# A group norm with channel attention: order of the high and value passes in the first pair and in steady passes, a statistics chain of four steps, and a last store in two halves from two queues

## Chip, cores and metric

The kernel runs on one core of a Trainium2 chip. The metric is the device time of one execution in microseconds, the median of several runs.

## What is computed

The input x has 16 images of 192 channels and 48 x 48 = 2304 positions. Per image, in eight heads of d = 24 channels:

```python
xn = _gn(x)                                  # 32 groups of 6 channels, eps 1e-5
qkv = tokens(xn) @ w_qkv                     # 2304 x 192 @ 192 x 576
q = q / norm(q, over the 2304 tokens)        # per channel
k = k / norm(k, over the 2304 tokens) * temperature
attn = softmax(k^T q, axis=-1)               # 24 x 24 per head
out = (attn applied to v) @ w_out + b_out
return x + out
```

## The kernel before, in words

Images go in pairs (8 pairs). Three tiles t hold a pair's 384 channels on 128 partitions: t = 0 and 2 the upper 128 channels of the two images, t = 1 the lower 64 of both. The normalised x is held as a sum of two 16-bit parts: `h_sb` (high) and `l_sb` (low = value - high). Attention between channels needs only the Gram matrix of the tokens, so the kernel computes, for a pair, the Gram matrix (`g_ps`), from it T = G W (`tq`, high and low), scores and norms, the softmax, V (`vh`, `vl`) and one folded matrix M (`mh0`, `mh1`, `ml0`, `ml1`) that is multiplied with the normalised x and added to x.

The work runs in nine steps p = -1 to 7, each written for all five engines at once. Step p has a first half A, 18 slots of 128 tokens, in which TensorE transposes tokens of pair p+1 into PSUM, ScalarE copies them (`tok`, line 613) and TensorE multiplies them into the Gram matrix, three slots behind; between slots stand the softmax, V and M of pair p. Its second half B has 18 results of pair p (384 columns each, VectorE line 938), and between them the small steps T, products, scores of pair p+1. The normalisation of pair p+2 runs beside both: in nine chunks of 768 columns, each needs a value pass `x<c>` (`xn`, line 566, a ring of three buffers), a high pass `h<c>` (line 575), both on ScalarE, and a low pass on GpSimd (line 503), which waits for both. The value passes 0 to 2 of the second pair are VectorE's (`second_value`, line 789). A value pass c must wait until low pass c-3 has read its buffer.

All engines execute in order. The order is written by hand in tables: `*_PE_A`, `*_ACT_A`, `*_VEC_A` give what stands behind which slot of half A, `*_B` what stands in half B; `FIRST_` is step -1, `SECOND_` step 0, `LAST_` step 7, the others are steady. `flip`, `v` and `m` on TensorE are the transposes of the scores, the V product and the M product. On VectorE `soft_in` (lines 853 to 858) needs `flip`; `exp` on ScalarE (line 619) needs the end of `soft_in`; `soft_out` (866 to 875) needs `exp`. `spread` (line 843) needs the powers that GpSimd takes of the norms (line 520).

Statistics: VectorE's `bn_stats` pieces (line 799) wait for a load of x; `channel_stats` (807 to 818) makes three 16-bit parts of mean and mean square, which TensorE sums over groups. SyncE issues loads, stores (line 408) and the copies `hl` of a tile's halves.

Of the kernel before, what the change touches and what calls it, by code (L numbers as in the profile page):

```python
# [107 lines left out]
def preact_attention(nc, x, w_qkv, temperature, w_out, b_out, ident, ident16, groups, headmask, out):  # L108
# [30 lines left out]
    with ExitStack() as ctx:  # L139
        def sb(name, shape, dt=F32):  # L140
            return ctx.enter_context(nc.sbuf_tensor(name, shape, dt))
# [218 lines left out]
        def _(sp):  # L360
# [355 lines left out]
        @block.vector
        def _(dve):
# [64 lines left out]
            def second_value(c):  # L782
# [164 lines left out]
            def step(p):  # L947
# [31 lines left out]
                for j in range(SLOTS):  # L979
                    for what in hooks(p, FIRST_VEC_A, VEC_A, LAST_VEC_A, PAIRS - 1).get(j, ()):  # L980
# [7 lines left out]
                    pieces(now, 0 if first else BN_A.get(j, 0))
                assert not now
                for n in range(NO):  # L990
                    if small:
                        result(p, n)
                    for what in hooks(p, FIRST_VEC_B, VEC_B, LAST_VEC_B, PAIRS - 2).get(n, ()):
# [406 lines left out]
```

## Time and profile before

| | us |
|---|---|
| median of 3 runs | 352.33 (351.12 to 352.65) |
| profiled execution, its own time | 350.15 |
| its span, first to last instruction | 348.4 |
| TensorE busy | 310.9 (89%) |
| VectorE busy | 284.4 (82%) |
| ScalarE busy | 242.9 (70%) |
| GpSimd busy | 145.8 (42%) |
| half A of step 0 begins | about 53 |
| first steady step begins | about 96 |

Times in the trace are from the start of the span. The device time holds 1.75 us around the span. A busy share is an average over stages; what a change in one stage is worth is read from the waits of that stage. PE is TensorE, PEld its weight loads, DVE VectorE, ACT ScalarE, POOL GpSimd, SP SyncE. The granted clock of TensorE is 0.988 of its full speed on the mean.

### The profile page before, as it was taken

The numbers are of one execution on the slowest core, as the hardware profiler recorded it, in microseconds if no ns is written. First come the engines' busy times: TensorE is split into PE (matmuls) and PEld (weight loads), VectorE is DVE, ScalarE is ACT, GpSimd is POOL, SyncE is SP. The second block draws the span as 40 slices with busy tenths as digits, with TensorE's granted clock in tenths as the row PEclk, the third lists the DMA queues.
The fourth block names the chain that finished last, engine by engine and source line by source line (L and its number), as shares of the span: only waits on it lengthen the run. The fifth ranks groups of instructions, "written<-read, shape, count | busy, mean of one in ns | idle before, by whom it ended". The sixth has DMA issues, their size and how long they took to land.

```text
span 348.4 us, 9368 instructions
## 1 busy us (share of the span) xinstructions
PE 310.9 (89%) x3692; PEld 221.8 (64%) x3692; DVE 284.4 (82%) x705; ACT 242.9 (70%) x447; POOL 145.8 (42%) x129
## 2 busy tenths in 40 slices
PE   0039858999999999999999999999999999999895
PEld 0027736765678667866787567866787568856552
DVE  5999894896999689986998699968998685278874
ACT  1089689867997599759996699759986899640300
POOL 0059679303870178315750287115930586002000
PEclk9999987999999999999999999999999999999999
DMA  7999920004995279915994399627992574016876
GB/s 225 355 322 259 246 77 2 3 1 144 301 350 164 92 208 349 301 52 169 305 310 127 119 292 328 216 93 186 320 322 63 154 235 132 3 48 181 283 215 229
DMA packets 30828, 67.75 MB, mean 194 GB/s; under 512 B 5504, under 2 KB 12096, under 8 KB 30784
## 3 DMA queue, kind: packets, MB, share of 16 engines
q1 hardware_dynamic: 30544, 66.56, 61.3%
q10 hardware_dynamic: 240, 0.59, 0.6%
q8 instruction: 29, 0.48, 0.6%
q14 instruction: 15, 0.12, 0.1%
HBM read 29.38 MB, written 28.31 MB: 166 GB/s over the span
## 4 chain that ended last, share of the span: by engine, by line
PE 72%; ACT 8%; issue 7%; DVE 6%; SPq 2%; DMA 2%; POOL 2%; ACTq 0%; POOLq 0%; DVEq 0%
PE u_ps L1015 29%; PE g_ps L1015 20%; PE s_ps L1015 10%; PE u_ps L1066 4%; PE u_ps L1067 4%; ACT tok L613 3%; ACT h_sb L575 2%; DMA wo<-in_L_conv_w_out_dram 2%; PE u_ps L1068 2%; PE u_ps L1069 2%; ACT xn L566 2%; DVE x_sb L938 1%; SPq L381 1%; POOL l_sb L503 1%; SPq L386 1%
## 5 line engine op out<-in xcount | busy, mean ns | idle before, releaser
L503 POOL TENSOR_TENSOR l_sb<-xn,h_sb 128x768 f16<-128x768 f32 x63 | 103.2, 1652 | 49.3 <-ACT h_sb L575 49.3
L938 DVE SCALAR_TENSOR_TENSOR x_sb<-u_ps,bias,x_sb 128x384 f32<-128x384 f32 x144 | 83.7, 610 | 13.6 <-PE u_ps L1015 13.0
L1015 PE MATMUL g_ps<-tok 128*128 128x64 f16 (+1 forms) x864 | 86.4, 240 | 4.1 <-ACT tok L613 4.0
L613 ACT COPY tok<-u_ps 128x384 f32<-128x384 f32 x144 | 65.7, 484 | 17.3 <-PE u_ps L1069 16.0
L799 DVE BATCH_NORM_STATS2 bnst<-x_sb 128x6 f32<-128x384 f32 x144 | 71.5, 545 | 4.0 <-DMA x_sb<-in_x_dram 3.9
L1015 PEld LDWEIGHTS g_ps<-tok 128*128 128x128 f16 x864 | 57.2, 99 | 27.5 <-ACT tok L613 6.5
L1015 PE MATMUL u_ps<-h_sb,ml 128*128 128x384 f16 (+1 forms) x336 | 72.7, 326 | 0.0
L566 ACT ACTIVATE xn<-x_sb,rb 128x768 f32<-128x768 f32 x60 | 59.6, 1026 | 14.0 <-POOL rb L515 14.0
L575 ACT ACTIVATE h_sb<-x_sb,rb 128x768 f16<-128x768 f32 x63 | 64.3, 1034 | 0.4 <-POOL rb L515 0.4
L1066 PE MATMUL u_ps<-id,h_sb 128*128 128x128 f16 x288 | 49.2, 224 | 6.1 <-DVE l_sb L779 5.3
L1067 PE MATMUL u_ps<-id,l_sb 128*128 128x128 f16 x288 | 49.2, 224 | 0.0
L1015 PE MATMUL u_ps<-hl,mh 128*128 128x384 f16 (+1 forms) x192 | 47.5, 330 | 0.1
L1015 PE MATMUL u_ps<-h_sb,mh 128*128 128x384 f16 (+1 forms) x192 | 47.1, 326 | 0.0
L509 POOL TENSOR_TENSOR grs<-gvar,minus_half 128x3 f32<-128x3 f32 x8 | 7.1, 882 | 95.6 <-DVE gvar L832 95.6
L1015 PE MATMUL u_ps<-l_sb,mh 128*128 128x384 f16 (+1 forms) x192 | 47.1, 326 | 0.0
L1015 PEld LDWEIGHTS u_ps<-h_sb,ml 128*128 128x128 f16 (+1 forms) x336 | 28.7, 101 | 20.1 <-issue 3.0
L1069 PE MATMUL u_ps<-id,l_sb 128*128 128x128 f16 x144 | 32.3, 224 | 0.0
L1068 PE MATMUL u_ps<-id,h_sb 128*128 128x128 f16 x144 | 32.3, 224 | 0.0
L1066 PEld LDWEIGHTS u_ps<-id,h_sb 128*128 128x128 f16 x288 | 27.5, 100 | 6.7 <-ACT h_sb L582 5.4
L1067 PEld LDWEIGHTS u_ps<-id,l_sb 128*128 128x128 f16 x288 | 28.9, 100 | 0.4
L1015 PEld LDWEIGHTS u_ps<-hl,mh 128*128 128x128 f16 (+1 forms) x192 | 14.7, 103 | 11.9 <-issue 3.1
L520 POOL TENSOR_TENSOR r<-n,minus_half 96x8 f32<-96x8 f32 x8 | 13.6, 1700 | 18.7 <-DVE n L837 18.7
(149 smaller groups left out, 527.0 us busy)
## 6 DMA issues: line engine op xcount, KB each, us to landing
x_sb<-in_x_dram SPq DMA_DIRECT2D x48, 384.0 KB, 5.5
out_dram<-x_sb SPq DMA_DIRECT2D x48, 384.0 KB, 3.5
out_dram<-x_sb SPq DMA_DIRECT2D x48, 192.0 KB, 3.2
x_sb<-in_x_dram SPq DMA_DIRECT2D x45, 192.0 KB, 5.0
hl<-h_sb SPq DMA_DIRECT2D x48, 96.0 KB, 3.2
hl<-l_sb SPq DMA_DIRECT2D x48, 96.0 KB, 3.4
x_sb<-in_x_dram ACTq DMA_DIRECT2D x3, 192.0 KB, 4.2
w<-in_L_conv_w_qkv_dram SPq DMA_DIRECT2D x1, 288.0 KB, 7.2
```

Source lines behind the costliest of these rows:

```text
L503: nc.gpsimd.tensor_tensor(l_sb[:, par, t, cols], xn[:, c % XN_RING, :], h_sb[:, par, t, cols], ALU.subtract).then_inc(l_ok, 1)
L520: nc.gpsimd.tensor_tensor(r8[:, :], n8[:, :], minus_half[0:HC, :].to_broadcast([HC, 8]), ALU.pow).then_inc(r8_ok, 1)
L566: nc.scalar.activation(xn[:, c % XN_RING, :], xcol(q, t, g * GW, GW), ACT.Identity, bias=rb[:, par, 1, t:t + 1], scale=rb[:, par, 0, t:t + ...
L575: nc.scalar.activation(h_sb[:, par, t, g * GW:g * GW + GW], xcol(q, t, g * GW, GW), ACT.Identity, bias=rb[:, par, 1, t:t + 1], scale=rb[:, ...
L613: nc.scalar.copy(tok[:, j % TOK_RING, :, :].rearrange("p b n -> p (b n)").bitcast(F32), slot_words(j)).then_inc(tok_a, 1)
L799: ins = V.bn_stats(bnst[:, t, 6 * part:6 * part + 6], xcol(q, t, part * BW, BW))
L938: V.scalar_tensor_tensor(out=xs, in0=block_ps(n), scalar=bias[:, t:t + 1], in1=xs, op0=ALU.add, op1=ALU.add).then_inc(out_ok, 1)
L1015: return nc.tensor.matmul(dst, lhs, rhs, start=start, stop=stop, skip_group_check=True)
L1066: nc.tensor.transpose(bank[:, b, 0:P], h_sb[:, par, 2 * b, px], id16[:, 0:P])
L1067: nc.tensor.transpose(bank[:, b, 256:384], l_sb[:, par, 2 * b, px], id16[:, 0:P])
L1068: nc.tensor.transpose(bank[:, :, P:P + C1], h_sb[:, par, 1, px], id16[:, 0:P])
L1069: nc.tensor.transpose(bank[:, :, P + C1:P + 2 * C1], l_sb[:, par, 1, px], id16[:, 0:P]).then_inc(tr_mm, 1)
```

## The change

Six things are edited. (1) In steady steps ScalarE's h7 moves from slot 4 to behind exp in slot 5, and h8 from slot 7 to slot 8. (2) In step -1 ScalarE takes T's high parts ahead of h2, and VectorE its third value pass behind T. (3) In step 0 the value passes 6 and 7 go from ScalarE to VectorE, so that h6, h7 and h8 come earlier on ScalarE, and flip, v and m stand two, one and one slots earlier on TensorE. (4) `channel_stats` keeps the moments as 32-bit numbers whose upper halves TensorE reads as the 16-bit parts: four dependent steps in place of six. (5) The last store, of tile 1 and the last 768 columns, is cut in two halves of 384 columns, each started as its result is done; SyncE issues the first image's part, ScalarE the second's. (6) The waits of GpSimd and of the ring follow (3).

```diff
-ACT_A = {1: ["h6"], 3: ["x8"], 4: ["h7"], 5: ["exp"], 7: ["h8"], 11: ["v"], 14: ["m"]}
+ACT_A = {1: ["h6"], 3: ["x8"], 5: ["exp", "h7"], 8: ["h8"], 11: ["v"], 14: ["m"]}
...
-FIRST_ACT_B = ["h0", "h1", "h2", "t2", "t0", "t1", "x3", "p", "h3", "x4", "h4", "x5"]
+FIRST_ACT_B = ["h0", "h1", "t2", "t0", "t1", "h2", "x3", "p", "h3", "x4", "h4", "x5"]
...
-FIRST_VEC_B = {0: ["var", "gram", "wm", "v0", "v1", "z", "v2", "t2", "t0"],
-               1: ["t1", "lo", "bn", "norms", "wo", "spread", "bn", "bn", "bn"]}
+FIRST_VEC_B = {0: ["var", "gram", "wm", "v0", "v1", "z", "t2", "t0"],
+               1: ["t1", "v2", "lo", "bn", "norms", "wo", "spread", "bn", "v6", "bn", "bn"]}
...
-SECOND_PE_A = {3: ["flip"], 10: ["v"], 13: ["m"]}
-SECOND_ACT_A = {0: ["h5"], 1: ["x6"], 2: ["h6"], 3: ["x7"], 4: ["h7"], 5: ["x8"], 6: ["exp"], 7: ["h8"], 12: ["v"], 15: ["m"]}
+SECOND_PE_A = {1: ["flip"], 9: ["v"], 12: ["m"]}
+SECOND_ACT_A = {0: ["h5"], 1: ["h6"], 2: ["h7"], 4: ["x8"], 5: ["exp", "h8"], 12: ["v"], 15: ["m"]}
+SECOND_VEC_A = {**VEC_A, 0: ["soft_in", "v7"]}
...
                 ch.then(V.tensor_tensor(mv[:, :, 1], mv[:, :, 1], msq[:, :], ALU.add))
-                ch.then(V.tensor_copy(parts[:, 0, :, :], mv[:, :, :]))
-                ch.then(V.tensor_tensor(res1[:, :, :], mv[:, :, :], parts[:, 0, :, :], ALU.subtract))
-                ch.then(V.tensor_copy(parts[:, 1, :, :], res1[:, :, :]))
-                ch.then(V.tensor_tensor(parts[:, 2, :, :], res1[:, :, :], parts[:, 1, :, :], ALU.subtract))
+                for k in (0, 1):
+                    ch.then(V.tensor_tensor(moments[:, k + 1, :, :], moments[:, k, :, :], parts[:, k, :, :], ALU.subtract))
...
+                        if p == PAIRS - 1 and k == NC_ - 1:
+
+                            for i in (0, 1):
+                                sp.wait_ge(out_ok, done[k] - 1 + i)
+                                chip, dram = ends([c + i * BW for c in at[g]], image, o_d, t, g * GW + i * BW, BW)[0]
+                                sp.dma_start(dram, chip).then_inc(stored[t][g], 16)
...
+            def last_store():
+                t, g = ROWS[-1]
+                q = PAIRS - 1
+                for i in (0, 1):
+                    c = g * GW + i * BW
+
+                    act.wait_ge(out_ok, (q + 1) * NO + NO - 1 + i)
+                    act.dma_start(o_d[2 * q + 1:2 * q + 2, P:C, c:c + BW].rearrange("o c n -> (o c) n"),
+                                  xcol(q, t, c, BW)[C1:P, :]).then_inc(stored[t][g], 16)
...
-                V.tensor_scalar(xn[:, c, :], xcol(1, t, g * GW, GW), rb[:, 1, 0, t:t + 1], rb[:, 1, 1, t:t + 1],
+
+                need(dve, l_ok, c + 1 - XN_RING)
+                V.tensor_scalar(xn[:, c % XN_RING, :], xcol(1, t, g * GW, GW), rb[:, 1, 0, t:t + 1], rb[:, 1, 1, t:t + 1],
```

ScalarE in a steady half A, from x8 to the copies behind h8; `tok` is a token copy, `xn` a value pass, `h_sb` a high pass, `s_ps` with 96x96 the exp. Before:

```order
L566 ACTIVATE xn<-x_sb,rb 128x768
L613 COPY tok<-u_ps 128x384
L575 ACTIVATE h_sb<-x_sb,rb 128x768
L613 COPY tok<-u_ps 128x384
L619 ACTIVATE s_ps<-s_ps 96x96
L613 COPY tok<-u_ps 128x384 x2
L575 ACTIVATE h_sb<-x_sb,rb 128x768
L613 COPY tok<-u_ps 128x384 x4
```

With the change:

```order
L575 ACTIVATE xn<-x_sb,rb 128x768
L622 COPY tok<-u_ps 128x384 x2
L628 ACTIVATE s_ps<-s_ps 96x96
L584 ACTIVATE h_sb<-x_sb,rb 128x768
L622 COPY tok<-u_ps 128x384 x3
L584 ACTIVATE h_sb<-x_sb,rb 128x768
L622 COPY tok<-u_ps 128x384 x3
```

The high pass that stood between two token copies now stands behind exp, and three copies follow it before h8 in place of two.

ScalarE in half A of step 0, from the first token copy's successor h5 on. Before:

```order
L575 ACTIVATE h_sb<-x_sb,rb 128x768
L613 COPY tok<-u_ps 128x384
L566 ACTIVATE xn<-x_sb,rb 128x768
L613 COPY tok<-u_ps 128x384
L575 ACTIVATE h_sb<-x_sb,rb 128x768
L613 COPY tok<-u_ps 128x384
L566 ACTIVATE xn<-x_sb,rb 128x768
L613 COPY tok<-u_ps 128x384
L575 ACTIVATE h_sb<-x_sb,rb 128x768
L613 COPY tok<-u_ps 128x384
L566 ACTIVATE xn<-x_sb,rb 128x768
L613 COPY tok<-u_ps 128x384
```

With the change:

```order
L584 ACTIVATE h_sb<-x_sb,rb 128x768
L622 COPY tok<-u_ps 128x384
L584 ACTIVATE h_sb<-x_sb,rb 128x768
L622 COPY tok<-u_ps 128x384
L584 ACTIVATE h_sb<-x_sb,rb 128x768
L622 COPY tok<-u_ps 128x384 x2
L575 ACTIVATE xn<-x_sb,rb 128x768
L622 COPY tok<-u_ps 128x384
L628 ACTIVATE s_ps<-s_ps 96x96
L584 ACTIVATE h_sb<-x_sb,rb 128x768
```

The value passes x6 and x7 are gone from between the token copies, the high passes have moved up, and behind exp stands h8 at once.

VectorE from the end of step -1 into step 0, from `spread` (`qk_s`) to the softmax; `xn` is a value pass. Before:

```order
L843 TENSOR_TENSOR qk_s<-s_ps,r 96x384
L799 BN_STATS bnst<-x_sb 128x6 x3
L853 TENSOR_TENSOR lg<-s_ps,mask 96x384
L855 TENSOR_REDUCE s_ps<-lg 96x96
L856 TENSOR_TENSOR s_ps<-s_ps,rk 96x96
L857 TENSOR_REDUCE mx<-s_ps 96x4
L858 TENSOR_TENSOR s_ps<-s_ps,mx 96x96
```

With the change:

```order
L863 TENSOR_TENSOR qk_s<-s_ps,r 96x384
L821 BN_STATS bnst<-x_sb 128x6
L811 TENSOR_SCALAR xn<-x_sb,rb 128x768
L821 BN_STATS bnst<-x_sb 128x6 x2
L873 TENSOR_TENSOR lg<-s_ps,mask 96x384
L875 TENSOR_REDUCE s_ps<-lg 96x96
L876 TENSOR_TENSOR s_ps<-s_ps,rk 96x96
L877 TENSOR_REDUCE mx<-s_ps 96x4
L878 TENSOR_TENSOR s_ps<-s_ps,mx 96x96
L811 TENSOR_SCALAR xn<-x_sb,rb 128x768
L821 BN_STATS bnst<-x_sb 128x6 x2
```

Value pass 6 now stands between the statistics pieces ahead of the softmax, and value pass 7 directly behind its last step.

## Rows read from the trace of the kernel before

**Rows 1.** The page: the chain that ended last, by engine.

```profile
PE 72%; ACT 8%; issue 7%; DVE 6%; SPq 2%; DMA 2%; POOL 2%; ACTq 0%; POOLq 0%; DVEq 0%
```

**Rows 2.** Windows: stretch, its length, busy us of PE, PEld, DVE, ACT, POOL, clock, DMA.

```profile
96.00:134.00 38.00, 37.75 (x464) 27.25 (x464) 33.02 (x84) 31.18 (x57) 17.94 (x15) 1.00 0.68 220
...
172.00:210.00 38.00, 37.37 (x459) 26.71 (x456) 32.45 (x82) 30.89 (x56) 17.27 (x15) 1.00 0.71 228
```

**Rows 3.** Waits from 58 to 96 us: total us, times, longest.

```profile
PEld g_ps L1015 <- ACT tok L613: 3.3, 7, 0.8
```

**Rows 4.** Timeline of TensorE, steady pass: start, us, instruction; Gram products 3, 4, 5.

```profile
99.83 0.60 PE L1015 MATMUL g_ps<-tok 128*128 128x384 f16 x6
...
100.60 0.60 PE L1015 MATMUL g_ps<-tok 128*128 128x384 f16 x6
...
101.79 0.62 PE L1015 MATMUL g_ps<-tok 128*128 128x384 f16 x6 [0.25 <-ACT tok L613]
```

**Rows 5.** Timeline of ScalarE at the same place: h7, token copy 5, exp.

```profile
100.31 1.06 ACT L575 ACTIVATE h_sb<-x_sb,rb 128x768 f16<-128x768 f32 x1
101.24 0.50 ACT L613 COPY tok<-u_ps 128x384 f32<-128x384 f32 x1
101.60 0.26 ACT L619 ACTIVATE s_ps<-s_ps 96x96 f32<-96x96 f32 x1
```

**Rows 6.** Timelines of VectorE (last softmax step) and GpSimd (low part 8).

```profile
100.51 0.26 DVE L858 TENSOR_TENSOR s_ps<-s_ps,mx 96x96 f32<-96x96 f32 x1
...
103.63 1.64 POOL L503 TENSOR_TENSOR l_sb<-xn,h_sb 128x768 f16<-128x768 f32 x1 [0.55 <-ACT h_sb L575]
```

**Rows 7.** Timeline of ScalarE, end of step -1: h3, first token copy of pair 1.

```profile
51.35 1.03 ACT L575 ACTIVATE h_sb<-x_sb,rb 128x768 f16<-128x768 f32 x1
...
55.04 0.46 ACT L613 COPY tok<-u_ps 128x384 f32<-128x384 f32 x1
```

**Rows 8.** VectorE: value passes (ns min/median/max, first and last start), spread, softmax's last step.

```profile
L789 DVE TENSOR_SCALAR xn<-x_sb,rb x3: 673/678/1732, 45.2 to 46.6; 128x768 f32<-128x768 f32 x3
...
56.08 0.55 DVE L843 TENSOR_TENSOR qk_s<-s_ps,r 96x384 f32<-96x384 f32 x1 [1.22 <-POOL r L520]
...
62.77 0.26 DVE L858 TENSOR_TENSOR s_ps<-s_ps,mx 96x96 f32<-96x96 f32 x1
```

**Rows 9.** Timeline of ScalarE, step 0: token copy 6, exp.

```profile
62.77 0.48 ACT L613 COPY tok<-u_ps 128x384 f32<-128x384 f32 x1
63.12 0.26 ACT L619 ACTIVATE s_ps<-s_ps 96x96 f32<-96x96 f32 x1
```

**Rows 10.** Timeline of TensorE, step 0: Gram products 6, 8, transposes 12, product 16, first result.

```profile
63.30 0.61 PE L1015 MATMUL g_ps<-tok 128*128 128x384 f16 x6 [0.34 <-ACT tok L613]
...
65.13 0.61 PE L1015 MATMUL g_ps<-tok 128*128 128x384 f16 x6
...
66.58 0.22 PE L1066 MATMUL u_ps<-id,h_sb 128*128 128x128 f16 x1
...
74.79 0.39 PE L1015 MATMUL g_ps<-tok 128*128 128x384 f16 x3 [0.68 <-ACT tok L613]
...
75.68 0.33 PE L1015 MATMUL u_ps<-h_sb,mh 128*128 128x384 f16 x1
```

**Rows 11.** Timeline of VectorE, step 3: last statistics step, first result.

```profile
190.87 0.17 DVE L818 TENSOR_TENSOR parts<-res,parts 128x6 bf16<-128x6 f32 x1
191.07 0.62 DVE L938 SCALAR_TENSOR_TENSOR x_sb<-u_ps,bias,x_sb 128x384 f32<-128x384 f32 x1
```

**Rows 12.** The end: last result, the two stores' issue, landing of the later one, a window.

```profile
344.06 0.62 DVE L938 SCALAR_TENSOR_TENSOR x_sb<-u_ps,bias,x_sb 128x384 f32<-128x384 f32 x1 [0.30 <-PE u_ps L1015]
...
344.71 1.11 SPq L408 DMA_DIRECT2D out_dram<-x_sb  x2
...
DMA to landing us min/median/max: 2.7/2.7/2.7
...
345.70:347.40 1.70, 0.00 (x0) 0.00 (x0) 0.00 (x0) 0.00 (x0) 0.00 (x0) 0.80 0.89 231
```

More of the change, by code:

```diff
@@ L90 @@
 POOL_SECONDS = (3, 5)
-BY_VECTOR_1 = 3
-SECOND_PE_A = {3: ["flip"], 10: ["v"], 13: ["m"]}
-SECOND_ACT_A = {0: ["h5"], 1: ["x6"], 2: ["h6"], 3: ["x7"], 4: ["h7"], 5: ["x8"], 6: ["exp"], 7: ["h8"], 12: ["v"], 15: ["m"]}
+BY_VECTOR_1 = (0, 1, 2, 6, 7)
+SECOND_PE_A = {1: ["flip"], 9: ["v"], 12: ["m"]}
+SECOND_ACT_A = {0: ["h5"], 1: ["h6"], 2: ["h7"], 4: ["x8"], 5: ["exp", "h8"], 12: ["v"], 15: ["m"]}
+SECOND_VEC_A = {**VEC_A, 0: ["soft_in", "v7"]}
 LAST_PE_A = {0: ["m"]}
@@ L174, in preact_attention @@
         bnst = sb("bnst", [P, 3, NB * 6])
-        mv = sb("mv", [P, 3, 2])
+        moments = sb("moments", [P, 3, 3, 2])
+        mv = moments[:, 0, :, :]
         msq = sb("msq", [P, 3])
-        parts = sb("parts", [P, 3, 3, 2], BF16)
-        res1 = sb("res1", [P, 3, 2])
-        res2 = sb("res2", [P, 3, 2])
+        parts = moments[:, :, :, :].rearrange("p a t s -> p (a t s)").bitcast(BF16).rearrange(
+            "p (a t s h) -> p a t s h", a=3, t=3, s=2)[:, :, :, :, 1]
         gsum = sb("gsum", [P, 3, 2])
@@ L311, in preact_attention @@
         out_ok = sem("out_ok")
-        STAT, GVAR, NORM, SOFT, ATTN = 6, 4, 2, 5, 6
+        STAT, GVAR, NORM, SOFT, ATTN = 4, 4, 2, 5, 6
         def high_count(k):
@@ L404, in step @@
                         t, g = ROWS[k]
-                        sp.wait_ge(out_ok, done[k])
-                        for chip, dram in ends(at[g], image, o_d, t, g * GW, GW):
-                            sp.dma_start(dram, chip).then_inc(stored[t][g], 16)
+                        if p == PAIRS - 1 and k == NC_ - 1:
[3 more added lines that the diff above has]
+                                sp.dma_start(dram, chip).then_inc(stored[t][g], 16)
+                        else:
+                            sp.wait_ge(out_ok, done[k])
+                            for chip, dram in ends(at[g], image, o_d, t, g * GW, GW):
+                                sp.dma_start(dram, chip).then_inc(stored[t][g], 16)
                     if more and k >= LOAD_LAG:
@@ L455, in _ @@
             for t, g in ROWS:
-                sp.wait_ge(stored[t][g], PAIRS * (32 if t == 1 else 16))
+                sp.wait_ge(stored[t][g], PAIRS * (32 if t == 1 else 16) + (32 if (t, g) == ROWS[-1] else 0))
         @block.gpsimd
@@ L498, in split @@
                     pool.wait_ge(h_ok, (q - 1) * NC_ + c + 1)
-                    if q == 1 and c < BY_VECTOR_1:
-                        pool.wait_ge(xn1_vec, c + 1)
-                    else:
-                        pool.wait_ge(xn_ok, (q - 1) * NC_ + c + 1 - BY_VECTOR_1)
+                    if q == 1 and c in BY_VECTOR_1:
+                        pool.wait_ge(xn1_vec, BY_VECTOR_1.index(c) + 1)
+                    else:
+                        by_vector = len(BY_VECTOR_1) if q > 1 else sum(k < c for k in BY_VECTOR_1)
+                        pool.wait_ge(xn_ok, (q - 1) * NC_ + c + 1 - by_vector)
                     nc.gpsimd.tensor_tensor(l_sb[:, par, t, cols], xn[:, c % XN_RING, :], h_sb[:, par, t, cols],
@@ L711, in step @@
                         small_steps[what](p + 1)
+            def last_store():
[6 more added lines that the diff above has]
+                                  xcol(q, t, c, BW)[C1:P, :]).then_inc(stored[t][g], 16)
             for_pairs(act, step)
+            last_store()
         @block.vector
@@ L979, in step @@
                 for j in range(SLOTS):
-                    for what in hooks(p, FIRST_VEC_A, VEC_A, LAST_VEC_A, PAIRS - 1).get(j, ()):
+                    for what in hooks(p, FIRST_VEC_A, VEC_A, LAST_VEC_A, PAIRS - 1, SECOND_VEC_A).get(j, ()):
                         if what == "stats":
@@ L985, in step @@
                             pieces(now, 1)
+                        elif what == "v7":
+                            second_value(7)
                         elif small:
@@ L1002, in step @@
                             mixed_weights()
-                        elif what in ("v0", "v1", "v2"):
+                        elif what in ("v0", "v1", "v2", "v6"):
                             second_value(int(what[1]))
```

## Prediction

> **What bounds the kernel now.** I read the page first. In its chain of what ended last TensorE holds 72% of the span, and no other engine more than 8% [rows 1]. The windows say where this holds: in a steady pass (96 to 134 us) TensorE is busy 37.75 of 38 us [rows 2]. So there only the gaps between matmuls can be won. In the pass of pair 0 the list of waits has the weight loads of Gram products waiting 3.3 us for ScalarE's copies of transposed tokens (`tok`), in 7 places [rows 3]. A steady pass has one such place. Gram products follow each other every 0.77 us (99.83, 100.60), but the one after is due at 101.38 and starts at 101.79 [rows 4]. ScalarE started the copy for it at 101.24, since a high part (h7, 0.93 us) stood ahead of it from 100.31 [rows 5]. Six steady passes (pairs 1 to 6) repeat this. The end is another stage: after VectorE's last result at 344.06 only the store is left [rows 12].
>
> **The change, part by part.** All sums are in the profiled execution, whose own time is 350.15 us for a span of 348.4; the median of the runs shown is 352.33 (351.12 to 352.65). I take the change in us from the one and subtract it from the other.
>
> *Steady passes: h7 goes behind exp, h8 one slot back.* Gram product 5's copy now starts at 100.31 and ends by 100.8: its 0.41 us wait is gone. Then comes exp. It needs VectorE's last softmax step, which starts at 100.51 and takes 0.26 [rows 6], so it ends at 100.77 and exp starts at some 100.86, where ScalarE stood free since 100.67. After it, exp holds the engine for 0.16 (0.26 in its row, less the 0.1 by which pieces overlap there) and h7 for 0.93 [rows 5]: the copy for Gram product 6 starts at 101.95 and, at 0.48, ends at 102.43. Product 6 is due at 101.38 + 0.77 = 102.15 and starts at 102.48. So a wait of 0.41 turns into one of 0.33: the stall moves by one product, 0.08 us is won, 0.5 in six passes. h8 then stands at some 103.03 and its low part on GpSimd at 104.1 in place of 103.63, ending 0.5 us later at 105.75 [rows 6]; the transposes that need it come behind Gram product 9 at about 106.2, so this costs nothing, with 0.45 us of cover left. Bounds: all 0.41 six times (2.5 us) if exp finds its input ready, a loss of 0.1 per pass if the copy is later than I count. I keep 0.5, since the row of the softmax step is that close.
>
> *First pass, T's high parts ahead of h2.* ScalarE has the same seven pieces and must wait for TensorE's T instead of running h2 in between. By my count the third product is cast by 51.4 as before, h3 starts at 51.38 against 51.35 and the first token copy at 55.07 against 55.04 [rows 7]. VectorE's part: of its three value passes the third (v2, at 46.6) took 1.73 us, as GpSimd's first low part ran beside it; the two before took 0.67 and 0.68 [rows 8]. Behind T it meets an idle GpSimd and should take 0.68. But GpSimd's third low part waits for v2 and ends at about 52.7; GpSimd has then another low part (1.64) before the power for the norms, which starts at 54.3, by my count 0.25 later than before. Sum for TensorE: 0 (the second pair's transposes are fed from copies at 55.04 either way), between -0.3 and +0.5.
>
> *Pass of pair 0.* ScalarE loses two value passes (x6, x7: 1.86 us), VectorE gets them (v6, v7), and h6, h7 come earlier. Step by step: the norms' spread on VectorE at 56.34 (was 56.08 [rows 8]); a statistics piece 0.47; v6 at 57.3, where GpSimd is in a low part (56.5 to 58.2). As with v2 I let v6 wait for its end and finish 0.42 later, at 58.6. Two pieces more and the softmax starts at 59.5. Its five steps take 2.3, so it ends at 61.8, where before its last step started at 62.77 and ended at 63.03 [rows 8]. ScalarE: token copies at 0.36 and three high parts bring it to x8 at 59.65; x8 needs GpSimd's sixth low part, at 60.15; the copy for product 5 starts at 61.1, exp at 61.87 (was 63.12 [rows 9]), h8, the copy for product 6 at 62.96 (was 62.77 [rows 9]), ending 63.44. So Gram product 6 starts at 63.5 against 63.30 [rows 10]: no gain yet. But then ScalarE holds nothing but copies. Before, the stretch from product 6 to the first result (75.68) was 12.38 us, in which TensorE waited 0.26 at product 8 (65.13, where two steps of 0.78 behind 63.30 make 64.87), 0.22 ahead of the transposes at 66.58, which want the last low part, and 0.68 for a copy queued behind M's high parts (74.79) [rows 10]. With low part 8 done at 65.6, and M's products two slots earlier in the same stretch (one slot for V's), these three are gone: 63.5 + 12.38 - 1.16 = 74.7. Gain 1.0 us, between 0.3 (v6 and v7 both meet a fresh low part of 1.64 us, and exp is late by as much) and 1.8 (neither does).
>
> Here the Trainium skill (SBUF — State Buffer, "Who interferes with whom") says that GpSimd and a VectorE instruction in a two-port mode lock each other out of a shared pair for a whole instruction, whichever starts second. The 1.73 against 0.68 us of the value pass agrees. By that rule v6 or v7, once started, also pushes GpSimd's next low part back by its own length.
>
> *Statistics chain, 6 steps to 4.* A step costs 0.20 (190.87 to 191.07 [rows 11]), so 0.41 per pass. In the head the first one is covered: the weights' load holds VectorE and ScalarE anyway; the second ends as TensorE reaches it, worth 0.05. In steady passes VectorE waits for the first result, so 0. Once, in the pass of pair 3, a load came late and the chain ran into the first result: 190.87 is followed by the result at 191.07 with no idle time [rows 11], and TensorE's busy time in that pass is 37.37 of 38 us in place of 37.75 [rows 2]. There up to 0.41 comes back, if the load is late again: I count 0.3.
>
> *Last stores.* After the last result (344.06 + 0.62) SyncE issued two DMAs, 1.11 us for both from 344.71; the later one landed 2.7 us after its start of 345.2, and data moved from 345.7 to 347.4 [rows 12]. Now half of it leaves 0.9 us earlier, and the last half is issued by two queues at once, at 344.75. With half the bytes, data moves from 345.7 for some 0.85 us, so the end comes 0.8 us earlier. Bounds: 0.5 (only the second issue is saved) to 1.3.
>
> The Trainium skill (SBUF — State Buffer, "Can I just issue two DMAs to hit both halves?") speaks against the second queue: two DMAs at partitions 0 and 64 share the same engines and serialize. By it the transfer is that half of 1.7 us, the 0.8 above; if they ran side by side it would be 1.2. No row here has two queues storing at once.
>
> Sum: 0.5 + 0 + 1.0 + 0.05 + 0.3 + 0.8 = 2.65 us. 352.33 - 2.65 = 349.7 us.
>
> **Rivals.**
> 1. *The value passes are not held.* v6 takes 0.68 in a gap of GpSimd; the softmax is 0.7 us earlier, x8 starts 0.3 earlier, product 6 starts at 62.8: 0.7 more, 349.0. For it: GpSimd's rows have gaps. Against: it has five low parts in a row there, and v2 met one.
> 2. *The gains vanish into new waits.* In pass 0 ScalarE stands still at exp with all token copies queued behind it; if v6 and v7 cost VectorE 1 us more, pass 0 gives 0.3, and the steady passes 0. Left are the tail and little else: 1.2 us, 351.1. For it: rows 6 leave exp only 0.1 us.
> 3. *Slower: exp holds the token copies in every pass.* ScalarE is in order, and exp now stands ahead of h7 without cover; before, h7 hid up to 0.8 us of softmax lateness (100.77 to 101.60). With lateness d the loss is d in each of seven passes. From d = 0.35 all of the 2.65 is gone, and at d = 0.65 it is 354.3, slower by over 0.5%. Against: the softmax hangs on the flip, which stands early in TensorE's order and waits for no copy of this pass.
> 4. *The change does less than it says:* the loads are on time (0 for 0.3), and the halves of the store serialize behind each other's issue (0.5): 350.3. This lies inside the main range.
>
> **How the numbers follow.** A change of 0.5% is 1.76 us, about what a measurement of this kernel can tell from none. Forecast as summed (with 4): 0.58, range 348.6 to 350.9. Rival 1: 0.14. Rival 2: 0.20. Rival 3: 0.08. Of the first, some 0.1 lies under 1.76 us of gain. Faster: 0.58 - 0.06 + 0.14 + 0.04 = 0.70; slower: 0.05; same: 0.25. The range that leaves out 2 in 10 reaches from 347.9 (rival 1 with a full tail and a fourth of the 2.5 that a steady pass could give at most) to 351.6 (rival 2 and half of its spread). 349.7 is the likeliest, not the mean.
>
> **What would show it.** Steady pass: the waiting Gram product is the one after h7, with a wait of 0.33, and a pass takes 0.08 us less. Pass 0: v6 or v7 longer than 1 us; Gram product 6 at about 63.5, first result at 74.7. v2 at 0.68 us and the first token copy at 55.0. Last store: two issues in two queues at the same time, the span's end 3.7 - 0.8 = 2.9 us after the last result. It is wrong if exp's input comes late in steady passes, if low part 8 stops the transposes, or if the head's copies start later than 55.1.

## The result, and the profile after

The changed kernel's median was 347.02 us (346.39 to 347.58, 4 runs) beside 351.73 for the kernel before (350.56 to 352.65, 4 runs); ratio 0.9867, 95% interval 0.9827 to 0.9908. Two later comparisons of the same pair gave 0.9894 (0.9853 to 0.9935) and 0.9910 (0.9878 to 0.9942). Over all comparisons of this study the changed kernel has 18 runs with a mean of 347.55 and the kernel before 101 runs with a mean of 351.03: **3.5 us faster, give or take 0.5** (two standard errors). I had forecast 349.7 (347.9 to 351.6), a gain of 2.65; both 347.02 and 347.55 lie under that range.

The profiled execution took 346.39 us for a span of 344.6. The page's chain that ended last has hardly moved: TensorE still holds it [rows 1].

```profile
PE 71%; DVE 9%; ACT 8%; issue 5%; DMA 2%; SPq 2%; POOL 2%; ACTq 0%; POOLq 0%; DVEq 0%
```

**Steady pass**, windows of two whole passes, from the first transposes of one pair to those of the next (the first line is the same cut in the kernel before; [rows 2] has it at other places):

```profile
96.08:133.92 37.84, 37.59 (x463) 27.16 (x462) 32.86 (x83) 31.12 (x56) 17.78 (x15) 1.00 0.68 219
...
94.69:132.37 37.68, 37.60 (x462) 27.16 (x461) 32.44 (x81) 31.12 (x56) 17.79 (x15) 1.00 0.71 222
132.37:170.06 37.69, 37.61 (x463) 27.15 (x462) 32.55 (x81) 31.13 (x56) 17.79 (x15) 1.00 0.69 215
```

TensorE works as long as before (37.60 for 37.59 us) and stands idle for 0.08 in place of 0.25. Gram products 4 to 6 in the first of the two passes [rows 4]:

```profile
99.21 0.60 PE L1037 MATMUL g_ps<-tok 128*128 128x384 f16 x6
...
99.99 0.60 PE L1037 MATMUL g_ps<-tok 128*128 128x384 f16 x6
...
101.00 0.61 PE L1037 MATMUL g_ps<-tok 128*128 128x384 f16 x6
```

ScalarE and VectorE there: exp, h7, token copy 6, and the softmax step that exp waits for [rows 5, 6]:

```profile
99.42 0.23 ACT L628 ACTIVATE s_ps<-s_ps 96x96 f32<-96x96 f32 x1
99.57 1.02 ACT L584 ACTIVATE h_sb<-x_sb,rb 128x768 f16<-128x768 f32 x1
100.49 1.22 ACT L622 COPY tok<-u_ps 128x384 f32<-128x384 f32 x3
...
99.13 0.26 DVE L878 TENSOR_TENSOR s_ps<-s_ps,mx 96x96 f32<-96x96 f32 x1
```

Products 4 and 5 follow each other in 0.78 us, product 6 comes after 1.01: the stall has moved to product 6, as forecast, but it is 0.24 us and not 0.33. The softmax step ends at 99.39 and exp starts at 99.42, 0.03 us later, where I had allowed 0.09. It is the same 0.03 in all six steady passes.

**Pass of pair 0**, Gram products 5 and 6 and the first result on TensorE, v6, the softmax's last step and v7 on VectorE, and two of GpSimd's low parts [rows 8 to 10]:

```profile
61.48 0.61 PE L1037 MATMUL g_ps<-tok 128*128 128x384 f16 x6
63.25 0.61 PE L1037 MATMUL g_ps<-tok 128*128 128x384 f16 x6 [0.82 <-ACT tok L622]
...
74.36 0.33 PE L1037 MATMUL u_ps<-h_sb,mh 128*128 128x384 f16 x1
...
57.18 1.31 DVE L811 TENSOR_SCALAR xn<-x_sb,rb 128x768 f32<-128x768 f32 x1
...
61.37 0.26 DVE L878 TENSOR_TENSOR s_ps<-s_ps,mx 96x96 f32<-96x96 f32 x1
61.54 0.67 DVE L811 TENSOR_SCALAR xn<-x_sb,rb 128x768 f32<-128x768 f32 x1
...
58.04 1.95 POOL L512 TENSOR_TENSOR l_sb<-xn,h_sb 128x768 f16<-128x768 f32 x1
...
62.36 1.64 POOL L512 TENSOR_TENSOR l_sb<-xn,h_sb 128x768 f16<-128x768 f32 x1 [0.75 <-DVE xn L811]
```

v6 was held beside GpSimd (1.31 us), v7 was not (0.67). One large stall is left, ahead of product 6, and behind it the copies keep pace: the first result starts at 74.36 (before 75.68 [rows 10]). Counted from the pass's first transposes (53.05 before, 52.99 now), product 6 starts at 10.25 us before and 10.26 now. So the gain of 1.33 lies behind product 6, as forecast: 1.27 up to the first result, the rest in the second half.

What lets the softmax start earlier is the flip. In the kernel before, VectorE was idle and waited for it:

```profile
60.74 0.55 DVE L853 TENSOR_TENSOR lg<-s_ps,mask 96x384 f32<-96x384 f32 x1 [2.73 <-PE s_ps L1194]
```

With the change this step starts at 59.35 and no longer waits. My prediction had the time right without naming this wait. No run takes the flip's move and that of the value passes apart.

**The end**, last result and the halves on two queues [rows 12]:

```profile
341.05 0.62 DVE L958 SCALAR_TENSOR_TENSOR x_sb<-u_ps,bias,x_sb 128x384 f32<-128x384 f32 x1 [0.29 <-PE u_ps L1037]
...
341.70 0.47 SPq L412 DMA_DIRECT2D out_dram<-x_sb  x1
341.70 0.50 ACTq L729 DMA_DIRECT2D out_dram<-x_sb  x1
...
DMA to landing us min/median/max: 2.1/2.1/2.1
...
DMA to landing us min/median/max: 2.4/2.4/2.4
```

Both last halves are issued at 341.70 and land after 2.1 us (SyncE's) and 2.4 us (ScalarE's). The span ends 3.55 us after the last result's start, before it was 4.34; spans are read to 0.1 us. Data of the last halves moved in this window (before, in [rows 12], the last data moved from 345.7 to 347.4):

```profile
342.80:343.70 0.90, 0.00 (x0) 0.00 (x0) 0.00 (x0) 0.00 (x0) 0.00 (x0) 1.00 0.78 219
```

### The profile page after: what moved, and what is told of

The parts are those of the page before. It is cut to its first block, busy times and chain, and to the rows that moved or that the text cites. A ratio compares the mean times of both kernels' runs of the same rounds, so it can differ in the third digit from the quotient of the medians.

```text
span 344.6 us, 9354 instructions
## 1 busy us (share of the span) xinstructions
PE 310.7 (90%) x3692; PEld 222.6 (65%) x3692; DVE 282.4 (82%) x691; ACT 241.8 (70%) x445; POOL 146.0 (42%) x129
## 4 chain that ended last, share of the span: by engine, by line
PE 71%; DVE 9%; ACT 8%; issue 5%; DMA 2%; SPq 2%; POOL 2%; ACTq 0%; POOLq 0%; DVEq 0%
PE u_ps L1037 33%; PE g_ps L1037 17%; PE s_ps L1037 12%; ACT tok L622 4%; ACT h_sb L584 3%; PE u_ps L1088 3%; PE u_ps L1089 3%; DMA wo<-in_L_conv_w_out_dram 2%; DVE bnst L821 2%; PE u_ps L1091 1%; PE u_ps L1090 1%; DVE l_sb L799 1%; DVE s_ps L786 1%; DVE xn L811 1%; SPq L382 1%
## 5 line engine op out<-in xcount | busy, mean ns | idle before, releaser
L512 POOL TENSOR_TENSOR l_sb<-xn,h_sb 128x768 f16<-128x768 f32 x63 | 103.1, 1653 | 51.5 <-ACT h_sb L584 49.1
L622 ACT COPY tok<-u_ps 128x384 f32<-128x384 f32 x144 | 64.2, 482 | 17.3 <-PE u_ps L1091 16.2
L575 ACT ACTIVATE xn<-x_sb,rb 128x768 f32<-128x768 f32 x58 | 57.5, 1026 | 14.4 <-POOL rb L524 14.0
```

What stands on the lines that cost most here:

```text
L512: nc.gpsimd.tensor_tensor(l_sb[:, par, t, cols], xn[:, c % XN_RING, :], h_sb[:, par, t, cols], ALU.subtract).then_inc(l_ok, 1)
L575: nc.scalar.activation(xn[:, c % XN_RING, :], xcol(q, t, g * GW, GW), ACT.Identity, bias=rb[:, par, 1, t:t + 1], scale=rb[:, par, 0, t:t + ...
L622: nc.scalar.copy(tok[:, j % TOK_RING, :, :].rearrange("p b n -> p (b n)").bitcast(F32), slot_words(j)).then_inc(tok_a, 1)
```

## The experiments

All comparisons are with the kernel before unless a line says otherwise. "First transposes" are those of each pair; their starts cut a trace into passes. The table has every trace but those of the three kernels with added steps or delayed loads, which come further down. Columns: start of the first transposes of pair 0; time from there to pair 1's (first pass); to pair 2's (pass of pair 0); the five steady passes that follow; last result's start to the end of the span (to 0.05, since spans are read to 0.1).

```
kernel       head   first  pair 0  steady passes (pairs 1 to 5)      end
before       23.86  29.19  43.03   37.84 37.84 38.51 37.84 37.83     4.34
e_same       23.70  29.19  43.30   37.84 37.84 37.83 37.84 37.84     4.31
e_chain      25.26  29.19  42.99   37.85 37.86 37.85 37.86 37.85     4.27
e_store      23.91  29.20  43.14   37.86 37.86 38.35 37.86 37.87     3.53
e_steady     25.20  29.20  43.05   37.68 37.69 37.67 37.68 37.68     4.30
e_pass0      24.08  29.19  41.54   37.85 37.84 38.85 38.02 37.85     4.26
e_first      23.75  29.23  44.04   37.85 37.84 39.21 37.84 38.18     4.33
e_first2     23.83  29.26  43.00   37.86 37.84 37.84 38.35 38.56     4.25
after        23.72  29.27  41.70   37.68 37.69 37.68 37.69 37.67     3.55
e_after2     25.95  29.27  41.67   37.66 37.67 37.66 37.66 37.66     3.55
e_after3     25.15  29.26  41.70   37.68 37.68 38.36 37.68 37.68     3.47
e_nofirst    25.07  29.20  41.48   38.36 37.68 37.67 38.67 37.68     3.54
best1        25.00  29.27  41.67   37.41 37.66 37.97 38.04 37.41     3.47
best2        24.12  29.26  41.41   37.41 37.41 37.42 40.75 37.42     3.51
best3        24.44  29.20  41.32   37.42 37.42 37.42 37.48 37.43     3.57
```

**Each part alone: e_chain, e_store, e_steady, e_pass0.** Each is the kernel before with one part of the diff and nothing else.

```diff
e_chain: STAT 6 -> 4, the parts read from moments' upper halves
e_store: the last k of SyncE's step in halves, last_store() on ScalarE
e_steady:
-ACT_A = {1: ["h6"], 3: ["x8"], 4: ["h7"], 5: ["exp"], 7: ["h8"], ...
+ACT_A = {1: ["h6"], 3: ["x8"], 5: ["exp", "h7"], 8: ["h8"], ...
e_pass0: BY_VECTOR_1, SECOND_PE_A, SECOND_ACT_A, SECOND_VEC_A, "v6" as in the change
```

> The kernel before with the statistics chain of four steps alone. Additive theory (each part gives what the two profiles show at its place): where loads are on time the chain is covered in every steady pass, the head gives 0.05 us, and only a pass with a late load gives up to 0.41; so 0 to 0.5 us below the kernel before, with pass starts as before except in a pass with a late load. Rival theory (the chain is what makes the medians differ by 4.7 where the profiles differ by 3.8): late loads come in several passes of ordinary runs, each gives up to 0.41, and the chain alone is worth 1 us or more.

Measured: ratio 0.9973 (0.9953 to 0.9994). In its trace no pass differs from those of before, where no load cost anything, by more than 0.04. The timed runs don't decide: the interval reaches from 0.2 to 1.7 us, and so takes in both theories.

> The kernel before with the last store in halves over two queues alone. Additive theory: 0.8 us below the kernel before, all of it after the last result (4.34 us from the last result's start to the span's end become 3.55, as in the profile of the changed kernel), and every pass start where it was. Rival: the second queue brings nothing or the end waits for the slower queue, 0.3 or less.

Measured: 0.9958 (0.9937 to 0.9980), 1.5 us by the ratio; in the trace the end took 3.53 us, 0.81 less than before. This run has halves and second queue together.

> The kernel before with h7 moved behind exp and h8 one slot back in the steady passes alone. Theory (the softmax's end wakes exp after 0.03 us, so the one stall shrinks from 0.41 to 0.24): 37.68 us per steady pass in place of 37.84, about 1.0 us in six passes. My prediction's count: 0.08 per pass, 0.5 in all. Rival (the 0.16 belongs to other parts, such as the shorter chain): 0 to 0.3 us.

Measured: 0.9971 (0.9946 to 0.9995); 37.68 in each of five passes, 0.16 less. That is all of the steady passes' gain in the changed kernel, so neither the chain nor another part has a share in it.

> The kernel before with the new order of the pass of pair 0 alone (x6 and x7 on VectorE as v6 and v7, the flip, V's and M's products earlier). Theory: 1.3 us, all between the first transposes of pair 1 and those of pair 2 (43.03 us become 41.7), nothing in the steady passes. My prediction's count: 1.0. Rival (part of that gain hangs on the earlier start that the first pass's reorder and the shorter chain give): 0.8 or less alone.

Measured: 0.9939 (0.9915 to 0.9964); the pass of pair 0 took 41.54 us, 1.49 less, more than in the changed kernel (41.70). The traces bear out the additive theory at each place. By the means of the timed runs the four parts add up to 5.7 us in place of 3.5. All four stand against the same 33 runs of the kernel before, whose mean (351.37) is 0.34 above that of all 101: four times that is 1.4 of the 2.2 us too many. The next runs ask what the comparison itself gives.

**The same kernel again: e_same, e_after2.**

> The kernel before, unchanged, run once more as if it were a changed one. It measures what the comparison itself gives: 0, give or take 0.7 us. The four parts run alone came out 1.25, 1.5, 1.0 and 2.0 us below the kernel before in their means, 5.7 in all, where the whole change gives 4.4 to 4.7. If this copy is also some 0.3 to 0.5 us below, that surplus is the comparison's own. Its trace also shows once more whether the pass of pair 3 runs into a late load (38.5 us or more in place of 37.84).

Measured: 0.9987 (0.9959 to 1.0014), by this ratio 0.45 us in its own favour, within the noise; no late load cost anything in its trace.

> The changed kernel once more, in more runs. Theory that the profiles tell all (3.8 us between the two profiled executions, and the 4.7 of the medians is spread): 3.8 or a little above. Theory that ordinary runs of the kernel before lose more to late loads than the profiled one did, and the four-step chain absorbs it: 4.4 or more, with the changed kernel's own runs closer together than those of before.

Measured: 0.9894, 3.7 us. Its trace shows why single runs stray: the head starts 2.2 us later than in the first trace of the same kernel. First the changed kernel's trace, then e_after2's; ScalarE's first cast of weights and TensorE's first transposes:

```profile
17.08 0.52 ACT L599 ACTIVATE wh<-w 128x384 f16<-128x384 f32 x1 [12.84 <-DMA wo<-in_L_conv_w_out_dram]
...
23.72 0.26 PE L1088 MATMUL u_ps<-id,h_sb 128*128 128x128 f16 x1 [5.25 <-DVE l_sb L799]
```

```profile
19.31 0.52 ACT L599 ACTIVATE wh<-w 128x384 f16<-128x384 f32 x1 [15.08 <-DMA wo<-in_L_conv_w_out_dram]
...
25.95 0.26 PE L1088 MATMUL u_ps<-id,h_sb 128*128 128x128 f16 x1 [5.25 <-DVE l_sb L799]
```

Between the two lines lie 6.64 us in both, and in every trace of the table. The weights' landing alone moves the start by 2.23, in kernels with and without the change (23.70 to 25.26 and 23.72 to 25.95 in the table). The span of e_after2 is 2.1 longer, and all of it is there. So the first comparison's 4.7 us, from four runs each, held about a microsecond of luck.

**The chain's slack: e_longchain, e_late6, e_late4.** The first has four more dependent steps.

```diff
-        STAT, GVAR, NORM, SOFT, ATTN = 6, 4, 2, 5, 6
+        STAT, GVAR, NORM, SOFT, ATTN = 10, 4, 2, 5, 6
...
+                for _ in range(4):
+                    ch.then(V.tensor_copy(res2[:, :, :], mv[:, :, :]))
```

> The kernel before with a statistics chain of ten steps in place of six (four more dependent copies, 0.82 us per pass). Theory: in a steady pass the chain has about 0.5 us of slack ahead of the first result, so each of the passes with a chain inside loses some 0.3 us more, 1.5 to 2 in the steady ones, 0.8 to 1.6 in the head, where a chain stands on the path: 2.5 to 3.5 us slower, and late loads then cost their full length. Rival (the chain never reaches the path in steady passes, so that the four-step chain can't have given anything there): slower by the head alone, 0.8 to 1.6 us.

Measured: 1.0101 (1.0069 to 1.0134), by this ratio 3.5 us slower; in its trace the first pass and the pass of pair 0 together took 1.4 more. VectorE ahead of the first result, in the kernel before and then in e_longchain:

```profile
113.90 0.17 DVE L818 TENSOR_TENSOR parts<-res,parts 128x6 bf16<-128x6 f32 x1
114.61 0.62 DVE L938 SCALAR_TENSOR_TENSOR x_sb<-u_ps,bias,x_sb 128x384 f32<-128x384 f32 x1 [0.55 <-PE u_ps L1015]
```

```profile
155.60 0.17 DVE L818 TENSOR_TENSOR parts<-res,parts 128x6 bf16<-128x6 f32 x1
155.80 0.79 DVE L820 COPY res<-mv 128x6 f32<-128x6 f32 x4
156.62 0.62 DVE L940 SCALAR_TENSOR_TENSOR x_sb<-u_ps,bias,x_sb 128x384 f32<-128x384 f32 x1
```

The idle 0.55 us is gone. The cleanest steady passes took 38.26 and 38.29 us, 0.42 and 0.45 more for 0.82 added, so the six-step chain had about 0.4 us of slack. (In these two passes VectorE also waited 0.2 and 0.3 us for a load; counted in, the slack is 0.6 to 0.7. So it is known as 0.4 to 0.7, and the idle 0.55 lies between.) The next two issue one load later in each pass, one with six steps and one with four:

```diff
-                    done_group = {2: 0, 5: 1, NC_ + LOAD_LAG - 1: 2}.get(k)
+                    done_group = {2: 0, 5: 1, NC_ + LOAD_LAG - 2: 2}.get(k)
```

> The kernel before, with the last load of each pair issued behind four copies of the queue in place of ahead of them (2.5 us of issues), so that it is late in every steady pass; chain of six steps. The ten-step chain took 0.43 us of its 0.82 from each on-time pass, so the chain has 0.4 us of slack. Theory: each pass loses the lateness less 0.4, some 1 to 2 us in each of five passes.

> The same late loads with the statistics chain of four steps. Theory (the two steps are slack that late loads eat): each late pass loses 0.41 us less than with six steps, 1.6 to 2.1 us less in all. Rival (the four-step chain gives nothing behind a late load, since VectorE's queue or the first result sets the restart): within 0.5 us of the six-step one.

Measured: 1.0104 (1.0060 to 1.0147) and 1.0060 (1.0032 to 1.0088): by the ratios the four-step chain is 1.5 us better behind late loads (1.8 by the medians), with intervals that overlap. How much a pass waits for its load is read in VectorE's waits. Here two of them, e_late6 from 252 to 270 us and e_late4 from 176 to 193:

```profile
DVE bnst L799 <- DMA x_sb<-in_x_dram: 1.6, 1, 1.6
```

```profile
DVE bnst L799 <- DMA x_sb<-in_x_dram: 2.9, 4, 1.1
```

Set against what the pass lost over 37.84 us, the five passes of each read:

```
e_late6 (six steps)   waited 2.0 0.8 1.3 1.6 1.6   lost 1.64 0.34 0.80 1.14 1.03   absorbed 0.36 to 0.57
e_late4 (four steps)  waited 0.2 0.7 2.9 1.2 2.8   lost 0.00 0.01 2.16 0.33 1.86   absorbed 0.74 to 0.94
```

(The last column leaves out the two waits that cost nothing.) The means are 0.47 and 0.85, 0.38 apart, for two steps removed of 0.41 us: in steady passes they add slack and nothing else. They pay only where the waits of a pass are longer than about 0.4, then up to 0.4. Other traces agree: the wait of 1.1 in the pass of pair 3 cost the kernel before 0.67, in the changed kernel a wait of 0.8 cost nothing.

**The first pass's new order: e_first, e_first2, e_nofirst.**

```diff
-FIRST_ACT_B = ["h0", "h1", "h2", "t2", "t0", "t1", "x3", ...
+FIRST_ACT_B = ["h0", "h1", "t2", "t0", "t1", "h2", "x3", ...
-FIRST_VEC_B = {0: [..., "z", "v2", "t2", "t0"], 1: ["t1", "lo", ...
+FIRST_VEC_B = {0: [..., "z", "t2", "t0"], 1: ["t1", "v2", "lo", ...
```

e_nofirst is the changed kernel with these lines as they were.

> The kernel before with the new order of T's high parts, the third high piece and the third value pass alone. The trace of the changed kernel has 29.27 us from the first transposes of pair 0 to those of pair 1 in place of 29.19. Theory (additive): the same 0.08 us more here, nothing elsewhere, so a result within the comparison's noise of 0.7 us. Rival (it is what lets the pass of pair 0 start its norms and softmax as it does): the pass of pair 0 changes by 0.3 us or more either way.

Measured: 1.0012 (0.9985 to 1.0039), and 44.04 us in the pass of pair 0. I had not foreseen a loss of 1.0. The windows show the clock. Kernel before, then e_first:

```profile
50.00:56.00 6.00, 5.18 (x70) 4.75 (x71) 4.39 (x10) 5.50 (x8) 5.00 (x3) 0.50 0.01 3
57.00:64.00 7.00, 5.62 (x75) 4.01 (x74) 4.14 (x11) 7.00 (x13) 5.76 (x4) 1.00 0.00 1
```

```profile
50.00:54.00 4.00, 2.70 (x66) 2.54 (x63) 3.62 (x8) 4.00 (x7) 2.94 (x2) 1.00 0.00 0
54.50:60.50 6.00, 5.05 (x40) 3.83 (x41) 2.50 (x6) 6.00 (x11) 5.92 (x5) 0.50 0.01 3
```

The granted clock (third number from the end of each row) is at the lower of its two levels (1.2 GHz) from 49.7 to 56.6 us in the kernel before; it fell while TensorE stood idle for 2.3 us (from 48.1) waiting for T. In e_first it is low from 54.2 to 61.1; idle times of 1.8 and 1.3 lay behind it, and a third, 1.3, had just begun. There the first four Gram products of pair 1 run at 1.03 to 1.06 us for six matmuls (before, the first alone took 1.04, the others 0.61), the flip comes at 61.23 in place of 60.21, and exp, behind it, holds the token copies: ScalarE waits 0.95 us for the softmax. This is the mechanism of my rival 3, in the old order and with the lower clock ahead of it.

> The kernel before with the first pass's new order alone, once more for one trace. In the first trace of it the granted clock was at its low level from 54.2 to 61.1 us, where the kernel before had it low from 49.7 to 56.6, and the pass of pair 0 took 44.04 us in place of 43.03. Theory (when the clock falls after TensorE's idle time in T differs from run to run, and the pass pays by how much of its Gram products stand in the low stretch): another fall, another length, 43.0 to 44.1. Rival (the new order itself puts the fall at 54 us): again a fall near 54 and 44.0.

Measured: one trace, low from 48.8 to 59.1, and 43.00 in the pass of pair 0. The order doesn't put the fall at 54 us; where it falls differs between executions of one kernel. Here it lay over three Gram products, over four in e_first.

> The changed kernel with the first pass's order of before. Theory (the new order of the first pass gives nothing, and costs 0.1 us by the later norms): 29.19 us in place of 29.27 in the first pass, the pass of pair 0 at 41.5 in place of 41.7, in all 0.2 us faster, which is within the noise of the comparison. Rival (the pass of pair 0 needs it): 0.3 us or more slower in the pass of pair 0.

Measured: 0.9910 (0.9882 to 0.9938), the same as the changed kernel beside it (0.9910). In the traces 29.20 against 29.27 in the first pass and 41.48 against 41.70 in the pass of pair 0: the new order costs 0.07 and some 0.2 us, as the theory had it at both places; the timed runs can't tell it.

**Better: best1, best2, best3.**

```diff
best1, from the changed kernel:
-ACT_A = {1: ["h6"], 3: ["x8"], 5: ["exp", "h7"], 8: ["h8"], ...
+ACT_A = {1: ["h6"], 3: ["x8"], 5: ["exp"], 6: ["h7"], 8: ["h8"], ...
best2, from best1:
-SECOND_ACT_A = {0: ["h5"], 1: ["h6"], 2: ["h7"], 4: ["x8"], 5: ["exp", "h8"], ...
+SECOND_ACT_A = {0: ["h5"], 1: ["h6"], 2: ["h7"], 5: ["x8"], 6: ["exp"], 7: ["h8"], ...
best3: best2 with the first pass's order of before
```

> The changed kernel with exp alone at its slot of the steady passes and h7 one slot later, behind the copy for Gram product 6. Theory (the stall of 0.24 is exp's hold of 0.15 and h7's 0.92 in one slot, which a single slot can't hide): in two slots both fit under the products' 0.77 each less a copy's 0.36 to 0.48 only in part; the stall falls to about 0.1 or to nothing and a steady pass to 37.45 to 37.6 us, 0.5 to 1.4 us faster than the changed kernel in six passes. Rival (h7 alone already overfills its slot as it did before, 0.41 of stall): 37.84 us per pass, 1 us slower than the changed kernel.

Measured: 0.9866 (0.9829 to 0.9902), 0.85 us under the changed kernel's median in the same comparison. A steady pass on time takes 37.41 us, so the stall is gone. But three of the five passes lost 0.25, 0.56 and 0.63 to late loads, for which VectorE had waited 1.0, 1.2 and 1.3.

> The changed kernel with exp in a slot of its own in the steady passes (best1) and in the pass of pair 0 too, there with x8, exp and h8 each one slot apart. Theory: of the stall of 1.0 us ahead of Gram product 6 in the pass of pair 0 some 0.4 to 0.8 us goes; then the last low part on GpSimd limits the transposes. 0.4 to 0.8 us below best1, 1.4 to 2 below the changed kernel. Rival (x8 behind another copy delays GpSimd's last low parts by as much as is won): as best1.

Measured: 0.9870 (0.9830 to 0.9910); the pass of pair 0 took 41.41 us, 0.26 less than in best1 and under the 0.4 expected at least. In its trace VectorE waited 3.7 us for loads in one pass, which cost 3.3; the timed median was 345.85.

> The kernel with exp in slots of its own (best2) and the first pass's order of before. Where no load is late: first pass 29.19, pass of pair 0 41.2 to 41.4, steady passes 37.41, so some 1.8 us below the changed kernel; of that late loads take back up to 0.6 in each pass in which one is over 0.8 us late, as they did in best1 (0.25, 0.56 and 0.63 in three passes). Expected in the timed runs: 0.7 to 1.8 us below the changed kernel.

> The changed kernel a third time, beside the two made from it, for a comparison on one chip: 3.3 to 4.7 us below the kernel before, as in its first two comparisons; steady passes of 37.66 to 37.69, pass of pair 0 41.7, the end 3.55 us after the last result's start.

Measured, on one chip: best3 0.9851 (0.9816 to 0.9886), e_after3 0.9910; medians 345.67 and 347.87, 2.2 us apart, above the 1.8 expected at most. best3's steady pass, with TensorE busy in all of it, and ScalarE's exp, copy 5, h7 and copies 6 and 7:

```profile
94.96:132.38 37.42, 37.42 (x463) 27.16 (x462) 32.45 (x81) 31.04 (x56) 17.80 (x15) 1.00 0.69 221
```

```profile
99.70 0.23 ACT L628 ACTIVATE s_ps<-s_ps 96x96 f32<-96x96 f32 x1
99.85 0.48 ACT L622 COPY tok<-u_ps 128x384 f32<-128x384 f32 x1
100.22 1.03 ACT L584 ACTIVATE h_sb<-x_sb,rb 128x768 f16<-128x768 f32 x1
101.14 0.84 ACT L622 COPY tok<-u_ps 128x384 f32<-128x384 f32 x2
```

exp's 0.15 and h7's 0.92 no longer stand between the same two copies. In this kernel ScalarE has room for either in a slot, not for both. For h7 the neighbours count too: before, it stood alone in its slot, but directly behind that of x8 (another 0.93 us), and cost 0.41.

## Why the prediction was wrong, step by step

The direction and the places held; the sum was 0.9 us short and its base too high. Predicted and measured, in us:

```
steady passes   0.5            1.0   (0.16 x 6; e_steady alone 0.16 per pass)
first pass      0 (-0.3, 0.5) -0.07
pass of pair 0  1.0 (0.3, 1.8) 1.33  (1.5 alone, less 0.2 that the first pass's order takes)
chain           0.05 + 0.3     0 (e_chain) + 0 to 0.67
last stores     0.8 (0.5, 1.3) 0.8
sum             2.65           3.1 to 3.7; timed 3.5 (3.0 to 4.0)
```

**The base.** "352.33 - 2.65 = 349.7": the three runs shown had a median 1.3 us above the mean of 101 runs, 351.03. I subtracted the gain from them though the profiled run was 350.15 and the three were 1.5 us apart. From 351.03 the same sum gives 348.4, inside the range. Of the 2.15 us between 349.7 and 347.55 this is the larger part (1.3); the terms make 0.85.

**Steady passes: mis-sized.** The step that failed is "it ends at 100.77 and exp starts at some 100.86". I took 0.09 us from softmax to exp in the pass of pair 0 [rows 8, 9]. But exp stood behind token copy 6 there (62.77 and 0.36 us), so the row showed the copy and not the wake-up. The clean reading stood in the same trace, in the last step, where ScalarE was idle ahead of exp:

```profile
320.07 0.26 DVE L858 TENSOR_TENSOR s_ps<-s_ps,mx 96x96 f32<-96x96 f32 x1
...
320.37 0.23 ACT L619 ACTIVATE s_ps<-s_ps 96x96 f32<-96x96 f32 x1 [9.01 <-DVE s_ps L858]
```

That is 0.03 to 0.04 us from end to start, as after the change (99.39 to 99.42, 61.63 to 61.67). That 0.06, a hundredth each from exp's hold (0.15 for 0.16) and h7's (0.92 for 0.93) and 0.02 from the copy's start to the product (0.51 for 0.53) make the stall 0.24 in place of 0.33, 0.08 more per pass, 0.5 in six. The mechanism (the stall moves by one product) was right; e_steady alone shows it, and best1, which parts the two pieces, removes the stall. Rival 3 rested on a lateness d of the softmax beyond my count. Counted, it ended 0.61 us ahead of product 5 (100.77 and 101.38); measured 0.60 (99.39 and 99.99), so d was 0. (Its sum was off too: seven times 0.35 is 2.45; all of the 2.65 is gone from d = 0.38.)

**Pass of pair 0: mis-sized by a third.** "ending 63.44. So Gram product 6 starts at 63.5": it started at 63.25. exp started 0.2 earlier than counted (61.67 for 61.87). v6's length was right (1.31; counted 57.3 to 58.6), but the whole pass began 0.06 earlier than in the trace that I counted from, the softmax was another 0.1 ahead (it ended at 61.63, counted 61.8), and exp woke 0.04 behind it, not 0.07; behind exp came 0.05 more. Then 0.1 came behind product 6 (11.11 us to the first result, forecast 11.2), and 0.07 in the second half of the pass, which I had not counted. All lies within the bounds that I gave.

v6 ended 0.41 us behind the low part that had begun ahead of it (56.44 to 58.08), as v2 had before (0.42). GpSimd's next low part took 1.95 us in place of 1.64. The rule of the Trainium skill (SBUF — State Buffer, "Who interferes with whom"), that whichever starts second waits, fits both. But GpSimd lost 0.31 there and not v6's own length of 0.67, which I had expected by that rule. The 0.75 us that GpSimd waited ahead of low part 7 is no such case: this part reads what v7 writes, and the row names v7 as what it waited for.

**First pass: right in effect.** v2 took 0.67 us behind T, as forecast. What it costs later was in my text as "0.25 later than before" for the norms, and I gave it no price; the table has it at 0.2 in the pass of pair 0 (e_pass0 and e_nofirst against the changed kernel).

**Chain: right in kind.** "if the load is late again: I count 0.3": e_late6 and e_late4 show the two steps as slack (0.38 by the traces). The 0.05 in the head does not show in e_chain's trace. In seven traces with six steps late loads cost 0.76 us per trace on average (0 to 1.7), in five with four steps 0.47 (0 to 1.7). That difference is 0.3, with a scatter larger than it; what the chain gives in an ordinary run stays open. The profiles happened to give 0.67 in one place, as before lost it and after did not.

**Last stores: right**, 0.79 in the change and 0.81 alone. I had counted 0.85 us in which the data of the last halves moves; it was 0.9, from 342.8 to 343.7. The same 0.8 can be split another way: the later of the two DMAs is issued 0.5 us earlier, since it no longer stands behind the other on one queue, and lands after 2.4 in place of 2.7. No run has the halves on one queue, so what the second queue gives by itself is not shown. The Trainium skill (SBUF — State Buffer, "Can I just issue two DMAs to hit both halves?") has two such DMAs serialize; by that I had 0.8, and 1.2 had they run side by side. The end fits the first. The landings, 2.1 and 2.4 us for two DMAs issued at the same moment, don't prove it.

**Rivals.** 1 (value passes not held) was half true: v7 was not, but v6, on which its gain hung, was. 2 (new waits eat the gain) fell. 3 fell in the changed kernel; its mechanism showed itself in one trace of e_first, through the clock. 4 was right on the chain where loads are on time (e_chain's trace) and wrong on the stores.

## What to carry to other kernels

A wait-free distance between producer and consumer must be read where nothing else stands ahead of the consumer on its in-order engine; otherwise the row shows that other work. When a stall is one in-order engine's piece in the wrong slot, count copy plus piece against the slot for each piece apart, and give a second piece a slot of its own. Look at what stands in the slot ahead, too. Subtract a gain from a mean over many runs, and find in two traces of one kernel which stage strays before reading a difference of 1% from four runs.

## What was unexpected

- Two executions of one kernel start their first transposes 2.2 us apart (23.72 and 25.95), with the landing of the weights' load (17.08 and 19.31).
- In or behind TensorE's idle time in T the clock falls, and it is low for 3.4 us (e_steady, from 51.8), 6.8 (before) or 10.2 (e_same, 49.1 to 59.4), by the execution. In the pass of pair 0, 43.03 us before, this cost 0.3 in e_same and nothing in e_first2 (both had three slow Gram products), but 1.0 in e_first with four.
- Once a steady pass has no stall left, late loads are what single passes still lose: waits of 1.0 to 1.3 us cost best1 0.25 to 0.63 a pass.
